# Moving on-chip tensors by 32 to 192 bytes, so that weights and streamed operands start at other distances modulo 256

## The reference

```
x = x + attention(layer_norm(ctx), modulated layer_norm(x))   # q from x; keys, values from both: 256 keys, 16 heads of 64
x = x + shared(layer_norm(x)) + routed(layer_norm(x))          # gated FFNs, 256 -> 704 -> 256; one expert of 8 per token
gated FFN:  (silu(x @ w1) * (x @ w3)) @ w2
```

## Time and profile before

| | us |
|---|---|
| median of 3 runs | 688.5 (688.04 to 688.54) |
| the profiled execution: its own time | 687.99 |
| its span, first to last instruction | 686.3 |
| TensorE busy | 675.2 |
| weight loads busy | 629.7 |
| VectorE, ScalarE, GpSimd busy | 470.6, 431.6, 271.7 |

### The profile page before, as it was taken

One profiled execution on the slowest core, in us unless ns is written; L12 is line 12 of the kernel. 1 busy time (PEld: TensorE's weight loads), 2 busy tenths in 40 slices (PEclk: granted clock), 3 DMA queues, 4 the chain that ended last, 5 costly groups with the idle time before them and its releaser, 6 DMA issues. The chain is left out here.

```text
span 686.3 us, 17910 instructions
## 1 busy us (share of the span) xinstructions
PE 675.2 (98%) x5935; PEld 629.7 (92%) x5936; DVE 470.6 (69%) x970; ACT 431.6 (63%) x1166; POOL 271.7 (40%) x428
## 2 busy tenths in 40 slices
PE   8899999999999999999999999999999999999997
PEld 8789899899998999989989988898899999999997
DVE  6787877877877788787797667366636676444443
ACT  4888888888788788888887864332434553222222
POOL 1853243252342343424557541047520454423333
PEclk9999999999999999999999999999999999999999
DMA  7645455555455445545546433003658999888870
GB/s 277 185 120 147 124 140 147 132 142 149 115 145 149 124 134 145 143 122 136 154 120 171 116 97 123 9 1 91 168 189 255 312 351 294 257 262 262 258 244 6
DMA packets 77935, 111.76 MB, mean 163 GB/s; under 512 B 28732, under 2 KB 45758, under 8 KB 77632
## 3 DMA queue, kind: packets, MB, share of 16 engines
q1 hardware_dynamic: 66016, 92.73, 45.4%
q0 software_dynamic: 8864, 18.38, 9.6%
q10 hardware_dynamic: 3008, 0.03, 0.3%
HBM read 63.74 MB, written 16.67 MB: 117 GB/s over the span
## 5 line engine op out<-in xcount | busy, mean ns | idle before, releaser
L1029 PE MATMUL PS<-BIG 128*128 128x256 f32 (+1 forms) x1164 | 199.1, 325 | 3.3 <-ACT V L630 2.4
L1029 PEld LDWEIGHTS PS<-BIG 128*128 128x128 f32 x1164 | 167.5, 192 | 20.2 <-issue 5.4
L648 ACT ACTIVATE PR<-PS,NMX 128x256 f32<-128x256 f32 x256 | 118.4, 475 | 40.9 <-DVE NMX L833 40.9
L2086 PE MATMUL PS<-XST,W 128*128 128x128 f32 x1012 | 116.7, 275 | 0.0
L491 POOL DMA_DIRECT2D PT<-PR x128 | 65.1, 514 | 126.2 <-DVE PR L845 82.1
L2086 PEld LDWEIGHTS PS<-XST,W 128*128 128x128 f32 x1012 | 115.0, 192 | 0.1
L657 ACT ACTIVATE PR<-PR,RINV 128x256 f32<-128x256 f32 x256 | 105.9, 509 | 0.0
L845 DVE STREAM_TRANSPOSE PR<-PR 128x512 f32<-128x512 f32 x124 | 82.0, 689 | 4.3 <-ACT PR L657 1.2
L833 DVE TENSOR_REDUCE NMX<-PS 128x4 f32<-128x1024 f32 x64 | 75.5, 1199 | 0.1
L1581 POOL DMA_INDIRECT out_x<-YS,WHO x23 | 31.7, 1376 | 85.0 <-DVE YS L1948 75.6
L1047 PE MATMUL PS<-KVF,WQ 128*128 128x128 f32 x512 | 63.8, 278 | 0.0
(11 more groups left out here) (187 smaller groups left out, 1105.2 us busy)
## 6 DMA issues: line engine op xcount, KB each, us to landing
PT<-PR SPq DMA_DIRECT2D x368, 64.0 KB, 2.3
W<-in_w SPq DMA_DIRECT2D x29, 640.0 KB
W<-in_w SPq DMA_DIRECT2D x21, 768.0 KB
PT<-PR POOLq DMA_DIRECT2D x128, 64.0 KB, 2.5
turned<-CXN SPq DMA_DIRECT2D x15, 256.0 KB, 2.0
INT<-turned POOLq DMA_DIRECT2D x56, 64.0 KB, 2.7
xs_sorted<-C SPq DMA_DIRECT2D x26, 128.5 KB, 3.1
W<-in_w SPq DMA_DIRECT2D x8, 352.0 KB
```

Of the source, the lines that this page charges most:

```text
L648: last = act.activation(probs, logits, ACT.Exp, bias=NMX[:, g, own, p % 2:p % 2 + 1], accum_out=SUM[:, p, own:own + 1])
L1029: last = pe.matmul(dst, stat(s, k), mov(m, k), start=n == 0, stop=n == len(todo) - 1)
L2086: last = pe.matmul(h[:, P * c:P * (c + 1)], lhs13(W13[par], k, c), XST[par][:, :, k, :], start=k == 0, stop=k == KD - 1)
```

## The change

BIG becomes 48 elements (192 bytes) longer. Within it MID and KQ move up by 64 bytes and KV by 192. Two dummy tensors are put in: SPACE, 8 elements (32 bytes), before the small tensors of the attention, and SPACE2, 24 elements (96 bytes), before XST in the experts. Nothing else differs: the instructions, their order, shapes and semaphores are the same.

```diff
+APART = 16
+SPACES = (8, 24)
-BIG_SIZE = 2 * (XT_SIZE + WS13_SIZE + FT * D + MID_SIZE + 2 * KV_SIZE)
+BIG_SIZE = 2 * (XT_SIZE + WS13_SIZE + FT * D + MID_SIZE + 2 * KV_SIZE) + 3 * APART
...
              "WS2": [view(FT * D, FT) for _ in range(2)]}
+    at[0] += APART
     mid = at[0]
     views["MID"] = [view(MID_SIZE, FT) for _ in range(2)]
+    at[0] += 2 * APART
     views["KV"] = [[view(KV_SIZE, KD) for _ in range(2)] for _ in range(2)]
...
         WOL = sb("WOL", [128, KC, D], FP32R)
+        sb("SPACE", [128, SPACES[0]])
         LNP = sb("LNP", [128, 4, KD])
...
         WHO = sb("WHO", [128, NT], I32)
+        sb("SPACE2", [128, SPACES[1]])
         XST = [sb(f"XST{i}", [128, 4, KD, 32]) for i in range(2)]
```

## The result

The changed kernel takes 684.28 us (median of 6 runs, 682.96 to 684.86) against 688.27 us (6 runs beside it): ratio 0.9939, 95% interval 0.9926 to 0.9951. It is faster, by 4.0 us (0.6%); 9.4 us were forecast, and the time lies 1.0 us above the range. Its profiled execution took 684.31 us, with a span of 682.6 us.

A forecast was written before the change was run, and what follows sets the result against it. TensorE's matmul count times pace was taken to bound the kernel. Keys 4.2, output projection 1.8, shared output 1.9 and routed output 1.7, less 0.2, gave 9.4 us gained: 679.1 us forecast, range 676.0 to 683.3.

The forecast's parts named there:

- What bounds the kernel: Whole kernel: nearly everywhere time is the number of matmuls times their pace; TensorE busy 98% of the span.
- The pace depends on the addresses: Dense TensorE stretches, 256 columns: 120 ns at distance 0, 118 at 32, 113 at 64, against the skill's read-port rule.
- rival 4: Dense matmuls: 113 ns comes from the quiet tail, not the distance, so time stays 688.5 us; chance 4%.
- Keys, 4.2 us: Attention keys, distance 0 to 64: 7 ns gained each, 3.9 us behind 45 us and 0.3 before, together 4.2 us.
- Output projection 1.8, shared output 1.9, routed output 1.7 us: These three products, moved to distance 64, step at 113 ns or gain 5 to 7 ns each: 1.8, 1.9, 1.7 us.
- Values, 0: Attention values, 512 columns, distance 0 to 192: no change taken; bounds 2.5 us gained to 5.0 us lost.
- rival 3: Attention values lose mildly, 1 to 5 us, giving 680 to 684 us; chance 5%.
- rival 1: Attention values gain as well at distance 192, 2.5 us more, giving 676.6 us; chance 13%.
- Plain float32 products, 0: Queries and routed hidden layer, 128 columns: no change taken; bounds 4.6 us gained to 12.2 us lost.
- rival 5: Values and half the routed hidden layer: distance 192 is worst, up to 13 ns more each, 690.7 us; chance 4%.
- What is late next: First routed tiles: weights arrive at queue pace; if slack is used up, 0.5 us of gain goes, kept for range.
- The second last projection: Tail's second last output projection, distance 64 to 192: may lose, at worst 0.1 us.

The follow-up runs named there:

- the maps: Kernels of matmuls alone, not the block: start addresses of stationary and moving operand varied; each ran once, 113.3 to 120 ns among paces at 256 columns.
- e_88: Changed kernel with the stationary operands of output projection, shared and routed output 24 bytes higher, at distance 88 instead of 64: 684.72 us, ratio 0.9941.
- e_keys0: Changed kernel with KV in front of MID in BIG, so keys and values are at distance 0 as before: 685.36 us, ratio 0.9962.
- after_light: Changed kernel loading only the first full chunk and short last one of the output weights of experts 3 to 7: 684.12 us, ratio 0.9947.
- e_keys_alone: Kernel before the change with KV alone moved up by 192 bytes, every other tensor keeping its remainder: 685.0 us, ratio 0.9949.
- e_best: e_88 with the keys' and queries' split tensors (KQ) back where the changed kernel has them: 682.33 us, ratio 0.9913.

## Why the prediction was wrong

- *What bounds the kernel*: right. TensorE's busy time fell by 3.8 us (675.2 to 671.4) and the span by 3.7; what is not busy stayed at 11 us.
- *The pace depends on the addresses, and the rule of the read ports in the Trainium skill (TensorE: Matmul & The Clock Gate, Part 2) does not hold*: right. One shape has 113.3 to 122 ns in the maps, at a granted clock of 1.00 with no other engine at work, and the keys went from 120 to 113.3 in the loop; rival 4 falls.
- *Keys, 4.2 us*: right, 3.7 us in the changed kernel, 3.9 us alone. All 28 sets behind 45 us went to 113.3. That was luck in part: distance 64 does not promise it, as 7 sets at the same addresses in e_88 show.
- *Output projection 1.8, shared output 1.9, routed output 1.7 us*: the step that failed. Measured are 0.12, 0.65 and 0.07 us. The prediction took the pace for a function of the distance and read its value at 64 from a single set of 10 steps. The maps show two steady paces there, 113.3 and 117.8 ns; which one a set falls into is decided by how it begins. e_keys0 shows it in the kernel: only the predecessor changed, and 118 became 113.5. The set of the earlier trace rows happened to begin well, and begins as well at 192 now. 5.4 us were forecast for these three terms and 0.8 came, 4.6 us of the miss of 5.4; the rest is the values, the wait for weights and 0.5 us of the keys, less what the start-up gave.
- *Values, 0*: a loss of 0.55 us, inside the bounds (rival 3's side, but under its 1 us); rival 1 falls. No distance measured is better than 0 for 512 columns.
- *Plain float32 products, 0*: right, 4.83 us for 44 before and after; rival 5 falls.
- *What is late next*: named with 0.5 us and kept out of the sum. It came: one tile waits 0.5 us in the changed kernel, three tiles 1.6 us in e_88. The size was right by luck. It was worked out as a gain of 75 ns a tile lost again, but the tiles gained nothing: they step by 6.92 us before and after. They start 4.2 us earlier (523.07 for 527.26 us), and with less to load (after_light) the wait is gone. The term belonged in the sum, since the rows already showed the queues full there.
- *The second last projection*: expected slower at 192; it kept 113 ns, as both distances have both paces.
- The start-up moves by 1 to 2 us from profile to profile (the first of the probabilities x values starts at 48.59 us before, 47.74 changed, 48.61 e_keys_alone, 49.63 e_88), so 0.85 us of the changed profile's 3.7 lie there, where 0.3 were forecast; a difference of 1 us in the whole span of one profile proves nothing. Behind the start-up the keys alone gained 3.0 us and the changed kernel 2.8: all its other placements together brought nothing there.
- *The attention from 45 to 394 us, about 5.5 us less*: from the output projection at 66.20 us to the one at 389.90 it was 323.7 us, and is 321.1 (65.15 to 386.25): 2.6 us less.

Why there is more than one pace is open. The trace has whole nanoseconds: the 113.3 shows as a cycle of 113, 113 and 114 ns, the 117.8 as 117 to 119. No set at 113.3 or 117.8 ns was seen to leave its pace again while its addresses stayed the same; what in the two reads decides the entry was not measured.

## What to carry to other kernels

When one pace is read from one short stretch, ask whether it is the only steady pace for these addresses: look for a second stretch with the same addresses and another beginning, or measure it with several beginnings. Do not take a map with a few beginnings for a promise either: 88 bytes had the short step four times out of four in the map, and 116.7 and 120 ns beside it in the kernels. Judge a placement by the sets of the kernel itself, one by one, and count the transient of the first 4 to 8 products. And when work moves earlier against loads whose DMA share is already 1, put the loss into the sum.

## What the runs showed of the hardware

- A product of 256 columns with a weight load of its own (FP32R, granted clock 1.00) steps by 113.3 to 122 ns, 6 to 15 ns above the 107 ns of the earlier trace rows, by the difference of the start addresses of stationary and moving operand modulo 256 bytes. Differences of 8 bytes count: 120.0 ns at 0, 115.5 at 8, 118.4 at 16. That the weight load and the moving stream hold each other up is the reading that fits; no run shows it by itself.
- Several distances have more than one steady pace for the same addresses, and how a set begins picks one: 113.3 and 117.8 ns at 64 and 192; 113.3, 116.7 and 120 at 88 (maps, e_88, e_best).
- With 512 columns the best step is 226.7 ns, at distance 0, which is among the worst for 256 columns.
- At the lower clock level the distance made no difference: at distance 64 the changed kernel took (3.19 - 0.415) / 13 = 213.5 ns (0.415 us is the last one's own duration, as in the earlier trace rows), at distance 0 it was 214 ns.

```profile
27.55 3.19 PE L1034 MATMUL PS<-BIG 128*128 128x256 f32 x14
```
